# Mixture-of-experts tiles whose second matrix is read in place, by an address in a register

## The chip, the cores and the metric

The kernel runs on one core of a Trainium2 chip. A core has five engines with queues of their own: TensorE (PE: matmuls, with PEld for its weight loads), VectorE (DVE), ScalarE (ACT), GpSimd (POOL) and SyncE (SP, which only starts transfers). The metric is the device time of one execution in microseconds.

## The reference

The computation is a stack of six layers on `x`, four sequences of 512 tokens of width 128. Each layer is `x = x + c * f(layernorm(x))`. Attention layers have 16 heads of width 8, with or without a causal mask. Two of the feed-forward layers are a mixture of experts: each of the 2048 tokens picks one of eight experts and goes through that expert's two matrices.

```python
logits = hn2 @ gate_w + gate_b
idx = jnp.argmax(logits, axis=-1)
mid = jax.nn.relu(jnp.einsum('th,ehf->etf', hn2, w1) + b1[:, None, :])
y = jnp.einsum('etf,efh->eth', mid, w2) + b2[:, None, :]
moe = y[idx, jnp.arange(hn2.shape[0])]
return x + moe.reshape(b, s, h)
```

`w1` is 8 x 128 x 512 and `w2` is 8 x 512 x 128. The other two feed-forward layers are dense, with low-rank additions.

## The kernel before, in words

**Stages.** A "batch" in the code is one sequence in one layer: numbers 0 to 3 are the first attention layer (its feed-forward part is the first mixture), 4 to 7 the second (causal), 8 to 11 the third (the second mixture), 12 to 15 the fourth (causal). The mixture is done in four halves of two sequences, 1024 tokens each: halves 0 and 1 stand between batches 3 and 4, halves 2 and 3 between batches 11 and the dense layer before batch 12.

**One half.** `gate`, `pick`, `rank` and `place` find for each token its expert and its place in a list sorted by expert, with every expert's tokens rounded up to tiles of 128. Up to 15 tiles (`SLOTS`) result. `place` has three parts on VectorE: part 0 counts the tiles of each expert (four instructions from L1012), part 1 makes each token's position (`pos`, L1022 to L1030), part 2 writes `owner`, the expert number of each of the 15 tiles (L1033 to L1041). Eight indirect transfers on POOL (`scatter`, L1236) write the token rows, each with its token's number in a 129th column, into `sorted`. Two transfers on SP (`xload`, L1282 and L1283) bring the sorted rows back into `sorted_rows`.

**One tile** then goes through:

- `lay` (VectorE, L1049): copies the tile's expert, 1156 columns of `w1`, `w2`, `b1` and `b2` laid side by side, from the resident `experts` into one of `NWE` = 3 slots of `we`. The expert's number is in a register, which VectorE loads one tile ahead from `owner` (`expert_of`, L854: a load, a register instruction and an assertion that it is in bounds).
- `tt` (TensorE, L696) transposes the tile's rows; ScalarE applies the norm's scale and bias to `hTm` (L797).
- `up` (TensorE, L701): four matmul instructions with `w1` from `we`. The profile lists each fp32 instruction twice, so a group has 8. ScalarE applies relu with `b1` (L804).
- `dn` (TensorE, L707): four matmul instructions with `w2` from `we`. VectorE then waits for a free result slot out of `NY` = 8, copies the tile's token numbers into `numbers_y` (L1057) and adds `b2` into `ysb` (L1058).
- `ysend` (POOL, L1241) sends the result's rows to `y_rows` by an indirect transfer with `numbers_y` as index.

When all tiles of a half are sent, SP loads the rows back (`yload`, L1289) and VectorE adds them to `x` (`yadd`, L1063).

**Order.** `schedule` (L250) makes one list of events out of due times. Due times are in quads, where one quad is a quarter of a batch's attention; `TILES_AT`, `ROUTE_AT`, `Y_AT`, `NEXT`, `DENSE_AT` and others hold them. `segment` (L187) merges events by due time with the attention steps. Each engine's program (`pe_program` L587, `act_program`, `dve_program`, `pool_program`, `sync_program`) walks the same list and issues its own part of each event, so the list fixes the order within each queue, and semaphores do the rest. `need` issues a wait unless the engine has already waited for as much. `tile_before(n, at, k)` is the tile k places earlier, whose slot is used again.

In the list of before, half 1 has the parts of `place` in the order 1, 2, 0 by due time (part 0 is due at 19.259, part 1 at 18.75), all of half 1's lays stand behind half 0's last `dn`, and half 2's last `dn` stands behind the first `tt` of half 3. The events that begin batch 4 (`stats`, `rstd`, `norm`, then `hT`, L601, `q`, `k`, `v`) stand between the tiles of half 1, `hT` behind `dn` of tile 2.

Of the kernel before, what the change touches and what calls it, by code (L numbers as in the profile page):

```python
# [40 lines left out]
NWE = 3  # L41
NY = 8
FLIPS = TOPK
WE = 2 * F + FB + P
# [34 lines left out]
PREP = [('stats', 7.927), ('rstd', 7.55), ('norm', 7.1), ('hT', 6.9), ('q', 6.7), ('qrem', 6.65), ('k', 6.419),  # L79
        ('krem', 6.553), ('qmid', 6.3), ('kmid', 6.1), ('qlo', 6.05), ('klo', 5.851), ('v', 2.951), ('keep',  # L80
        -2.776)]
# [5 lines left out]
SECOND = [('hT', 1.871), ('q', 1.3), ('qrem', 1.25), ('k', 1.15), ('krem', 1.1), ('qmid', 1.0), ('kmid', 0.9),  # L87
        ('qlo', 0.94), ('klo', 0.8), ('v', -1.0), ('keep', -7.0)]
SECOND_STACK, SECOND_EVERY = 1.056, 0.182
# [3 lines left out]
        1.05), ('stats', 1, 1.2), ('rstd', 1, 1.2), ('norm', 1, 1.5), ('v', 0, 2.0)], 12: [('stats', 0, 0.207),  # L93
        ('rstd', 0, 0.0), ('norm', 0, 0.35), ('hT', 0, 0.5), ('q', 0, 0.65), ('qrem', 0, 0.7), ('k', 0, 0.8),
        ('krem', 0, 0.85), ('qmid', 0, 0.9), ('kmid', 0, 1.0), ('qlo', 0, 1.0), ('klo', 0, 1.05), ('stats', 1, 1.2),
        ('rstd', 1, 1.2), ('norm', 1, 1.5), ('v', 0, 3.334)]}
FLIP_AT = 15.132
# [4 lines left out]
STACK_FROM, STACK_EVERY = 6.412, 0.253  # L102
# [3 lines left out]
LOADS_FROM, LOADS_EVERY = 2.931, 0.418  # L106
# [6 lines left out]
        13.45, 'xfold': 13.65, 'lnorm': 13.9, 'lT': 14.4, 'gate': 14.8}, 3: {'lstats': 17.25, 'lrstd': 17.25,  # L113
# [7 lines left out]
        'lnorm': 6.3, 'lT': 6.8}, 13: {'lstats': 9.85, 'lrstd': 9.85, 'lnorm': 10.3, 'lT': 10.8}, 14: {'lstats':  # L121
        15.25, 'lrstd': 15.25, 'lnorm': 15.7, 'lT': 16.2}, 15: {'lstats': 17.65, 'lrstd': 17.48, 'lnorm': 17.88,
        'lT': 18.13}}
ROUTE_AT = {0: {'pick': 11.1, 'rank': 11.6, 'place0': 11.8, 'place1': 12.0, 'place2': 12.2, 'scatter': 12.209,
        'every': 0.15, 'xload': 15.2}, 1: {'pick': 18.304, 'rank': 18.5, 'place0': 19.259, 'place1': 18.75,
        'place2': 18.95, 'scatter': 18.8, 'every': 0.005, 'xload': 20.0}, 2: {'pick': 27.1, 'rank': 27.6, 'place0':
        27.8, 'place1': 28.189, 'place2': 28.389, 'scatter': 28.3, 'every': 0.15, 'xload': 31.2}, 3: {'pick': 34.2,
        'rank': 34.5, 'place0': 34.55, 'place1': 34.598, 'place2': 34.9, 'scatter': 34.362, 'every': 0.005, 'xload':
        36.0}}
# [5 lines left out]
Y_AT = {0: {'yload': 20.072, 'yadd0': 20.582, 'yadd1': 20.682}, 1: {'yload': 23.882, 'yadd0': -0.468, 'yadd1':  # L135
        -0.221}, 2: {'yload': 36.197, 'yadd0': 36.597, 'yadd1': 36.697}, 3: {'yload': 39.75, 'yadd0': 40.093,
        'yadd1': 40.123}}
DENSE_AT = {8: {'at': 39.75, 'unit': 0.26, 'fdn': 1.05}, 9: {'at': 40.764, 'unit': 0.273, 'fdn': 1.063}, 10: {'at':
        41.843, 'unit': 0.273, 'fdn': 1.011}, 11: {'at': 44.011, 'unit': 0.221, 'fdn': 1.05}, 12: {'at': 14.2,
        'unit': 0.121, 'fdn': 1.05, 'send': 1.3}, 13: {'at': 15.391, 'unit': 0.26, 'fdn': 1.05, 'send': 1.3}, 14:  # L140
        {'at': 16.9, 'unit': 0.26, 'fdn': 1.05, 'send': 1.3}, 15: {'at': 18.4, 'unit': 0.26, 'fdn': 1.05, 'send':
        1.3}}
NEXT_AT = {4: {'at': 20.651, 'stack': 0.801, 'every': 0.152}, 12: {'at': 41.47, 'stack': 0.801, 'every': 0.136}}


def tiles_of(hm):

    T, jobs = TILES_AT[hm], []
    for t in range(SLOTS):
        up = T["start"] + T["every"] * t  # L150
        jobs += [(up - (T["lay0"] if t < 2 else T["lay"]), "lay", hm, t), (up + T["tt"], "tt", hm, t),
                 (up, "up", hm, t), (up + T["dn"], "dn", hm, t), (up + T["ysend"], "ysend", hm, t)]
    return jobs
# [13 lines left out]
def sums(hm):  # L167
    return [(Y_AT[hm][f"yadd{b}"], "yadd", 2 * hm + b, None) for b in range(2)]

# [79 lines left out]

def schedule(causal_of):  # L250
# [22 lines left out]
    return plan + segment([12, 13, 14, 15], causal_of, jobs)  # L273


def program(nc, d):
    with ExitStack() as ctx:
# [63 lines left out]
        experts = sb("experts", [P, E, WE])  # L341
# [23 lines left out]
        numbers_y = sb("numbers_y", [P, NY], U32)  # L365
# [187 lines left out]
        def number_of(hm, t):  # L553
            return hm * SLOTS + t
# [31 lines left out]

        def pe_program(pe):  # L587
            for ev in plan:
# [108 lines left out]
                elif name == "up":  # L697
                    need(pe, b_free, at_b[("tt", n, at)] + 1)
# [30 lines left out]
        def act_program(a):  # L729
            for ev in plan:  # L730
# [68 lines left out]
                elif name == "up":  # L799
                    if tile_before(n, at, 2):  # L800
                        need(a, a_full, at_a[("dn", *tile_before(n, at, 2))] + 1)
                    for fb in range(FB):
                        at_ = number_of(n, at) % NWE
                        ins = a.activation(mid_e[:, number_of(n, at) % 2, fb, :], b_tiles(o)[:, fb, :], ACT.Relu,  # L804
                                           bias=we[:, at_, 2 * F + fb:2 * F + fb + 1])
# [33 lines left out]
        def dve_program(v):  # L839
# [11 lines left out]
            def expert_of(eng, hm, t):  # L851

                k_ = SLOTS * (hm % 2) + t
                return eng.value_load(owner[0:1, k_:k_ + 1], min_val=0, max_val=E - 1)  # L854

            next_expert = {}
            for ev in plan:
# [173 lines left out]
                elif name == "place":  # L1031
# [11 lines left out]
                    next_expert[n] = expert_of(v, n, 0)  # L1043
                elif name == "lay":
# [4 lines left out]
                    v.tensor_copy(we[:, number_of(n, at) % NWE, :], experts[:, bass.ds(next_expert[n], 1), :]  # L1049
                                  .rearrange("p o c -> p (o c)")).then_inc(laid, 1)  # L1050
                    if at + 1 < SLOTS:
                        next_expert[n] = expert_of(v, n, at + 1)
                elif name == "dn":
                    r = number_of(n, at) % NY
                    if tile_before(n, at, NY):
                        need(v, y_sent[r], 16 * (number_of(n, at) // NY))
                    v.tensor_copy(numbers_y[:, r:r + 1], sorted_rows[n % 2][:, at, P:ROW].bitcast(U32))  # L1057
                    v.tensor_tensor(ysb[:, r, :], pair_of(ka)[:, 0, 0:P],  # L1058
                                    we[:, number_of(n, at) % NWE, 2 * F + FB:WE], ALU.add).then_inc(a_free, 1)
# [94 lines left out]
        def pool_program(g_):  # L1154
            for ev in plan:
# [274 lines left out]
```

## Time and profile before

| | us |
|---|---|
| median of 3 runs | 1014.93 |
| lowest and highest | 1014.77, 1016.52 |
| the profiled execution | 1020.19 |
| its span (first to last instruction) | 1018.4 |
| TensorE busy in the span | 897.5 |
| VectorE busy in the span | 779.7 |
| ScalarE busy in the span | 674.8 |

The profile is of one execution, 5.26 us above the median; its granted TensorE clock averages 0.966 of full speed. Times of rows are counted from the start of the span. In a row of an engine's list, the bracket behind it gives the idle time of that engine before it and what ended the idle time; an arrow points from what is written to what is read. "issue" means that the profile shows nothing that the engine waited for, and "remote" or "another core or an unknown queue" that the event which released it has no visible source.

### The profile page before, as it was taken

The numbers are of one execution on the slowest core, as the hardware profiler recorded it, in microseconds if no ns is written. First come the engines' busy times: TensorE is split into PE (matmuls) and PEld (weight loads), VectorE is DVE, ScalarE is ACT, GpSimd is POOL, SyncE is SP. The second block draws the span as 40 slices with busy tenths as digits, with TensorE's granted clock in tenths as the row PEclk, the third lists the DMA queues.
The fourth block names the chain that finished last, engine by engine and source line by source line (L and its number), as shares of the span: only waits on it lengthen the run. The fifth ranks groups of instructions, "written<-read, shape, count | busy, mean of one in ns | idle before, by whom it ended". The sixth has DMA issues, their size and how long they took to land.

```text
span 1018.4 us, 25342 instructions
## 1 busy us (share of the span) xinstructions
PE 897.5 (88%) x10020; PEld 477.1 (47%) x10020; DVE 779.7 (77%) x1412; ACT 674.8 (66%) x1470; POOL 342.2 (34%) x603
## 2 busy tenths in 40 slices
PE   2699999898778799999899999889698989999998
PEld 1123333236767455554323333249685645555465
DVE  5889899855447887888989999817368788888646
ACT  2288887786555577777798878786362358767631
POOL 4444312242646323233232312516571133311100
PEclk8599999999989899999999999999799989999999
DMA  5117740001133221121010200010310222110000
GB/s 146 46 44 178 191 107 2 16 10 47 43 94 85 78 66 35 35 66 43 23 46 22 55 11 2 23 41 30 97 33 24 62 64 65 33 38 4 3 22 21
DMA packets 60520, 52.29 MB, mean 51 GB/s; under 512 B 9106, under 2 KB 57362, under 8 KB 60402
## 3 DMA queue, kind: packets, MB, share of 16 engines
q1 hardware_dynamic: 48980, 40.00, 14.6%
q10 hardware_dynamic: 8478, 4.62, 2.2%
q0 software_dynamic: 2944, 6.05, 1.8%
q8 instruction: 79, 1.29, 0.6%
q14 instruction: 39, 0.32, 0.1%
HBM read 13.64 MB, written 11.06 MB: 24 GB/s over the span
## 4 chain that ended last, share of the span: by engine, by line
PE 53%; DVE 21%; issue 10%; ACT 10%; another core or an unknown queue 2%; DMA 2%; POOL 1%; DVEq 1%; ACTq 0%; SPq 0%; POOLq 0%
PE ps L576 14%; PE ps L652 13%; DVE negm L937 10%; ACT pt L770 7%; PE ps L715 4%; PE ps L607 3%; PE ps L707 3%; PE ps L701 3%; PE ps L582 3%; DVE blockm L928 2%; PE ps L721 2%; PE ps L660 2%; PE ps L612 1%; PE ps L670 1%
## 5 line engine op out<-in xcount | busy, mean ns | idle before, releaser
L770 ACT ACTIVATE pt<-ps 128x512 f32<-128x512 f32 (+1 forms) x896 | 458.3, 567 | 156.1 <-PE ps L576 107.2
L937 DVE TENSOR_REDUCE negm<-ps 128x2 f32<-128x1024 f32 x256 | 300.9, 1219 | 31.0 <-PE ps L576 28.4
L652 PE MATMUL ps<-pt,va 128*32 128x256 f32 (+1 forms) x4352 | 274.3, 341 | 12.1 <-ACT ot L776 5.5
L928 DVE TENSOR_REDUCE blockm<-ps 128x8 f32<-128x1024 f32 (+1 forms) x192 | 195.2, 1042 | 34.2 <-PE ps L576 21.8
L576 PE MATMUL ps<-ks,qs 61*128 61x128 bf16 (+2 forms) x1536 | 174.0, 293 | 35.7 <-DVE negm L937 16.0
L576 PE MATMUL ps<-qs,ks 64*128 64x128 bf16 (+3 forms) x1408 | 168.1, 296 | 7.8 <-ACT pt L770 2.3
L652 PEld LDWEIGHTS ps<-pt,va 128*32 128x32 f32 x4352 | 91.9, 108 | 124.5 <-issue 83.0
L576 PEld LDWEIGHTS ps<-ks,qs 61*128 61x128 bf16 x1536 | 54.8, 95 | 189.8 <-issue 86.6
L1206 POOL CAST mpart<-negm 128x16 bf16<-128x16 f32 x64 | 13.2, 207 | 300.2 <-DVE negm L937 153.8
L804 ACT ACTIVATE stage<-ps,pt 128x128 f32<-128x128 f32 x240 | 68.6, 373 | 41.6 <-PE ps L701 29.8
L1241 POOL DMA_INDIRECT y_rows<-pt,numbers_y x60 | 70.7, 1179 | 63.4 <-DVE pt L1058 55.0
L576 PEld LDWEIGHTS ps<-qs,ks 64*128 64x128 bf16 x1408 | 57.9, 94 | 63.7 <-ACT pt L770 47.0
L701 PE MATMUL ps<-hTm,pt 128*128 128x128 f32 x480 | 68.0, 287 | 15.0 <-DVE pt L1049 12.9
L707 PE MATMUL ps<-pt,stage 128*128 128x128 f32 x480 | 66.5, 283 | 4.5 <-ACT stage L804 3.4
L701 PEld LDWEIGHTS ps<-hTm,pt 128*128 128x128 f32 x480 | 61.4, 200 | 19.0 <-ACT hTm L797 12.0
L1146 POOL TENSOR_TENSOR q<-q,parts 128x512 f32<-128x512 f32 x29 | 33.5, 1156 | 95.0 <-ACT parts L752 94.9
L1049 DVE COPY pt<-experts 128x1156 f32 x60 | 46.7, 785 | 24.0 <-PE ps L652 17.6
L707 PEld LDWEIGHTS ps<-pt,stage 128*128 128x128 f32 x480 | 61.0, 199 | 6.1 <-issue 4.5
L715 PE MATMUL ps<-hTa,wk 128*128 128x512 f32 x128 | 58.6, 599 | 2.3 <-DVE stage L1070 1.6
L810 ACT ACTIVATE stage<-ps 128x512 f32<-128x512 f32 x32 | 19.1, 597 | 37.2 <-PE ps L715 32.4
L797 ACT ACTIVATE hTm<-ps,wpk 128x128 f32<-128x128 f32 x60 | 28.2, 472 | 21.2 <-remote 12.3
L607 PE MATMUL ps<-hT,wpk 128*128 128x512 f32 x64 | 39.0, 699 | 1.7 <-ACT hT L743 0.9
(151 smaller groups left out, 1017.9 us busy)
## 6 DMA issues: line engine op xcount, KB each, us to landing
qs<-parts SPq DMA_DIRECT2D x80, 128.0 KB
ks<-parts SPq DMA_DIRECT2D x77, 128.0 KB
experts<-in_experts SPq DMA_DIRECT2D x8, 578.0 KB, 6.3
sorted<-stage ACTq DMA_DIRECT2D x4, 967.5 KB, 8.3
qs<-mrow SPq DMA_DIRECT2D x128, 6.0 KB
pt<-y_rows SPq DMA_DIRECT2D x8, 256.0 KB, 2.9
qs<-parts SPq DMA_DIRECT2D x32, 56.0 KB
ks<-parts SPq DMA_DIRECT2D x30, 56.0 KB
```

The source lines that it names most:

```text
L576: ends[s] = pe.matmul(banks[s][:, col:col + c1 - c0], stationary[s][:, i * P:(i + 1) * P], moving[s][:, c0:c1], start=(m_ == 0), stop=(not ...
L607: pe.matmul(b_bank(o), w["w" + name], hT[:, :], start=True, stop=True).then_inc(b_full, 1)
L652: ins = pe.matmul(pv_bank[32 * j:32 * j + 32, q0:q1], va[n % 2][:, kb, value_at(g, j):value_at(g, j) + 32], pt[:, k_, from_:from_ + q1 - q ...
L701: ins = pe.matmul(b_tiles(o)[:, a, :], we[:, number_of(n, at) % NWE, a * P:(a + 1) * P], hTm[:, number_of(n, at) % 2, :], start=True, stop ...
L707: ins = pe.matmul(pair_of(ka)[:, 0, 0:P], mid_e[:, number_of(n, at) % 2, a, :], we[:, number_of(n, at) % NWE, F + a * P:F + (a + 1) * P], ...
L715: pe.matmul(pair_of(ka)[:, 0, :] if kx else b_bank(o), wk[:, kx, at * P:(at + 1) * P], hTa[:, n % 2, :], start=True, stop=True).then_inc(a ...
L770: a.activation(pt[:, k_ % NPT, S * s:S * s + width], b_bank(o + s)[:, 0:width], ACT.Exp).then_inc(b_free, 1)
L804: ins = a.activation(mid_e[:, number_of(n, at) % 2, fb, :], b_tiles(o)[:, fb, :], ACT.Relu, bias=we[:, at_, 2 * F + fb:2 * F + fb + 1])
L928: v.tensor_reduce(blockm[:, g % 2, :, t, PLACES[c_]], pair_of(ka)[:, :, 0:width].rearrange("p s (b c) -> p s b c", c=P), AX, ALU.max, nega ...
L937: v.tensor_reduce(negm[:, g % 2, :, t, c_], pair_of(ka), AX, ALU.max, negate=True).then_inc(a_free, 1)
L1049: v.tensor_copy(we[:, number_of(n, at) % NWE, :], experts[:, bass.ds(next_expert[n], 1), :] .rearrange("p o c -> p (o c)")).then_inc(laid, 1)
L1241: g_.indirect_dma_start(d["y_rows"][n], bass.IndirectOffsetOnAxis(numbers_y[:, r:r + 1], 0), ysb[:, r, :], None).then_inc(y_sent[r], 16)
```

## The change

The second matrix is no longer copied by `lay`. It stays in `experts`, and each `dn` matmul reads it there at an address that is worked out from a register. For that, TensorE loads all 15 expert numbers of a half in one go, ahead of the half's first `up`; VectorE does the same at the end of `place` part 2, in place of one number per tile. `lay` copies 644 columns into one of 5 slots. Results have 15 slots, one for each tile of a half, and `numbers_y` goes: `ysend` reads the index straight from the 129th column of `sorted_rows`. The load of half 2's sorted rows therefore waits until half 0's results have been sent. The weights are packed in another order on the host, with the same bytes. A check at build time (`in_order`) fixes the order of the routing steps and of the counted events, and the due times are set anew.

```diff
-NWE = 3
-NY = 8
+NWE = 5
+NY = SLOTS
-WE = 2 * F + FB + P
+WE = F + FB + P
+W2_AT = WE
...
-        experts = sb("experts", [P, E, WE])
+        experts = sb("experts", [P, E, WE + F])
...
+        def experts_of(engine, hm):
+
+            k_ = SLOTS * (hm % 2)
+            return nc.values_load_multi_w_load_instructions(owner[0:1, k_:k_ + SLOTS], engines=[engine], min_val=0,
+                                                            max_val=E - 1)[1]
...
                 elif name == "up":
+                    if at == 0:
+                        need(pe, owner_step, 3 * n + 3)
+                        expert[n] = experts_of(mybir.EngineType.PE, n)
...
                     for a in range(FB):
+                        w2 = experts[:, bass.ds(expert[n][at], 1), W2_AT + a * P:W2_AT + (a + 1) * P]
                         ins = pe.matmul(pair_of(ka)[:, 0, 0:P], mid_e[:, number_of(n, at) % 2, a, :],
-                                        we[:, number_of(n, at) % NWE, F + a * P:F + (a + 1) * P], start=(a == 0),
-                                        stop=(a == FB - 1))
+                                        w2.rearrange("p o c -> p (o c)"), start=(a == 0), stop=(a == FB - 1))
...
                     v.wait_ge(owner_step, 3 * n + 3)
-                    next_expert[n] = expert_of(v, n, 0)
+                    expert[n] = experts_of(mybir.EngineType.DVE, n)
...
-                    v.tensor_copy(we[:, number_of(n, at) % NWE, :], experts[:, bass.ds(next_expert[n], 1), :]
+                    v.tensor_copy(we[:, number_of(n, at) % NWE, :], experts[:, bass.ds(expert[n][at], 1), 0:WE]
                                   .rearrange("p o c -> p (o c)")).then_inc(laid, 1)
-                    if at + 1 < SLOTS:
-                        next_expert[n] = expert_of(v, n, at + 1)
...
-                    v.tensor_copy(numbers_y[:, r:r + 1], sorted_rows[n % 2][:, at, P:ROW].bitcast(U32))
...
-                    g_.indirect_dma_start(d["y_rows"][n], bass.IndirectOffsetOnAxis(numbers_y[:, r:r + 1], 0),
+                    g_.indirect_dma_start(d["y_rows"][n], bass.IndirectOffsetOnAxis(sorted_rows[n % 2][:, at, P:ROW]
+                                                                                      .bitcast(U32), 0),
...
                     elif n == 2:
-                        need(sp, a_free, at_a[("dn", 0, SLOTS - 1)] + 1)
+                        for r in range(NY):
+                            need(sp, y_sent[r], 16 * len(range(r, SLOTS, NY)))
```

What the due times move, in the order of the list: half 0's lays run two tiles earlier; half 1's `place` goes in the order 0, 1, 2; its first lays stand ahead of half 0's last `dn`; batch 4's `hT` stands behind `dn` of tile 4, `k` behind tile 5, `v` behind tile 12; half 2's last `dn` stands ahead of half 3's first `tt`. The rest, shown in part, moves by a tile or a step of attention at most:

```diff
-        1.05), ('stats', 1, 1.2), ('rstd', 1, 1.2), ('norm', 1, 1.5), ('v', 0, 2.0)], 12: [('stats', 0, 0.207),
+        1.05), ('stats', 1, 1.2), ('rstd', 1, 1.2), ('norm', 1, 1.5), ('v', 0, 2.267)], 12: [('stats', 0, 0.207),
-LOADS_FROM, LOADS_EVERY = 2.931, 0.418
+LOADS_FROM, LOADS_EVERY = 2.751, 0.418
-        'rank': 34.5, 'place0': 34.55, 'place1': 34.598, 'place2': 34.9, 'scatter': 34.362, 'every': 0.005, 'xload':
+        'rank': 34.5, 'place0': 34.55, 'place1': 34.58, 'place2': 34.9, 'scatter': 34.362, 'every': 0.005, 'xload':
-TILES_AT = {0: {'start': 16.75, 'every': 0.207, 'lay0': 0.35, 'lay': 0.384, 'tt': -0.257, 'dn': 0.22699999999999998,
-        'ysend': 0.277}, 1: {'start': 20.401, 'every': 0.207, 'lay0': 0.35, 'lay': 0.384, 'tt': -0.213, 'dn':
-        0.22699999999999998, 'ysend': 0.216}, 2: {'start': 32.681, 'every': 0.207, 'lay0': 0.35, 'lay': 0.214, 'tt':
+TILES_AT = {0: {'start': 16.75, 'every': 0.207, 'lay0': 0.35, 'lay': 0.719, 'tt': -0.257, 'dn': 0.22699999999999998,
+        'ysend': 0.277}, 1: {'start': 20.088, 'every': 0.207, 'lay0': 0.358, 'lay': 0.392, 'tt': -0.213, 'dn':
+        0.22699999999999998, 'ysend': 0.216}, 2: {'start': 32.628, 'every': 0.207, 'lay0': 0.35, 'lay': 0.304, 'tt':
-        'lay': 0.363, 'tt': -0.257, 'dn': 0.22699999999999998, 'ysend': 0.277}}
+        'lay': 0.268, 'tt': -0.257, 'dn': 0.22699999999999998, 'ysend': 0.548}}
```

## Rows read from the trace of the kernel before

**Rows 1.** The profile page: the engines' busy time, the chain by engine.
```profile
PE 897.5 (88%) x10020; PEld 477.1 (47%) x10020; DVE 779.7 (77%) x1412; ACT 674.8 (66%) x1470; POOL 342.2 (34%) x603
...
PE 53%; DVE 21%; issue 10%; ACT 10%; another core or an unknown queue 2%; DMA 2%; POOL 1%; DVEq 1%; ACTq 0%; SPq 0%; POOLq 0%
```

**Rows 2.** Table of windows: busy us of each engine, clock, DMA share, GB/s.
```profile
270.00:290.00 20.00, 10.74 (x61) 9.62 (x62) 5.76 (x17) 5.46 (x19) 11.47 (x12) 0.74 0.31 93
290.00:326.00 36.00, 31.08 (x258) 28.63 (x258) 22.34 (x73) 23.94 (x75) 23.82 (x20) 1.00 0.29 82
...
712.00:732.00 20.00, 11.13 (x67) 10.25 (x66) 4.45 (x12) 6.19 (x21) 12.01 (x12) 0.78 0.32 94
```

**Rows 3.** Table of waits: engine, line, releaser; us in total, times, longest.
```profile
DVE numbers_y L1057 <- remote: 16.2, 5, 6.1
...
PE ps L701 <- DVE pt L1049: 12.9, 9, 4.2
```

**Rows 4.** Engine lists, half 0 into 1: start, us, work, [idle before <- releaser].
```profile
259.79 1.46 POOL L1241 DMA_INDIRECT y_rows<-pt,numbers_y  x1 [1.33 <-DVE pt L1058]
...
270.87 1.13 PE L701 MATMUL ps<-hTm,pt 128*128 128x128 f32 x8 [1.01 <-DVE pt L1049]
...
273.79 0.68 PE L701 MATMUL ps<-hTm,pt 128*128 128x128 f32 x4 [0.90 <-DVE pt L1049]
...
279.27 2.04 PE L707 MATMUL ps<-pt,stage 128*128 128x128 f32 x8 [3.20 <-ACT stage L804]
...
285.10 0.15 DVE L1057 COPY numbers_y<-stage 128x1 uint32<-128x1 uint32 x1 [2.52 <-remote]
...
286.27 2.04 PE L701 MATMUL ps<-hTm,pt 128*128 128x128 f32 x8 [4.22 <-DVE pt L1049]
```

**Rows 5.** Instructions of L1049, then of L1057: ns least/median/most.
```profile
L1049 DVEq FUSED_REGOPS  x60: 57/57/65, 238.8 to 756.8; - x60
L1049 DVE COPY pt<-experts x60: 730/763/1552, 238.9 to 756.9; 128x1156 f32 x60
...
L1057 DVE COPY numbers_y<-stage x30: 145/154/155, 244.4 to 727.9; 128x1 uint32<-128x1 uint32 x30
```

**Rows 6.** VectorE's list at place0; POOL's behind half 1's last scatter.
```profile
271.75 0.21 DVE L1012 SCALAR_TENSOR_TENSOR more<-ranks,count 128x64 f32<-128x64 f32 x1
...
277.30 0.96 POOL L1241 DMA_INDIRECT y_rows<-pt,numbers_y  x1 [0.30 <-issue]
...
285.73 1.22 POOL L1241 DMA_INDIRECT y_rows<-pt,numbers_y  x1 [1.92 <-DVE pt L1058]
```

**Rows 7.** TensorE's list: batch 4's first transposes, between tiles of half 1.
```profile
297.78 0.66 PE L601 MATMUL ps<-identf,lnx 128*128 128x128 f32 x4 [2.38 <-DVE lnx L897]
```

**Rows 8.** TensorE's list, half 2 into half 3.
```profile
721.71 0.47 PE L696 MATMUL ps<-identf,pt 128*128 128x128 f32 x1 [5.67 <-DMA pt<-sorted]
...
721.98 1.92 PE L707 MATMUL ps<-pt,stage 128*128 128x128 f32 x8
...
729.08 1.34 PE L701 MATMUL ps<-hTm,pt 128*128 128x128 f32 x8 [3.04 <-DVE pt L1049]
```

**Rows 9.** The chain of waits behind half 2's place part 2: start, us, what.
```profile
641.42 0.31 DVEq L854
...
641.77 0.19 DVEq L854
...
642.00 0.02 DVEq L854
...
642.06 0.36 DVE rc L945
```

**Rows 10.** Engine lists: behind half 0's place part 2, and its first up.
```profile
195.41 2.36 DVE L937 TENSOR_REDUCE negm<-ps 128x2 f32<-128x1024 f32 x2 [0.95 <-DVE owner L1041]
...
240.03 1.06 PE L701 MATMUL ps<-hTm,pt 128*128 128x128 f32 x8
```

**Rows 11.** The chain of waits, half 2 into half 3.
```profile
715.45 6.05 another core or an unknown queue
```

More of the change, by code:

```diff
@@ L77 @@
 LEAD = 2.0
[L79 to L81 removed]
+PREP = [('stats', 7.927), ('rstd', 7.55), ('norm', 7.1), ('hT', 6.967), ('q', 6.767), ('qrem', 6.717), ('k', 6.486),
+        ('krem', 6.62), ('qmid', 6.3), ('kmid', 6.1), ('qlo', 6.05), ('klo', 5.851), ('v', 2.951), ('keep', -2.776)]
 HEAD = [("stats", 0), ("rstd", 0), ("norm", 0), ("stats", 1), ("rstd", 1), ("clear", 0), ("hT", 0), ("q", 0), ("qrem", 0),
@@ L124 @@
+        'lnorm': 17.88, 'lT': 18.13}}
 ROUTE_AT = {0: {'pick': 11.1, 'rank': 11.6, 'place0': 11.8, 'place1': 12.0, 'place2': 12.2, 'scatter': 12.209,
-        'every': 0.15, 'xload': 15.2}, 1: {'pick': 18.304, 'rank': 18.5, 'place0': 19.259, 'place1': 18.75,
-        'place2': 18.95, 'scatter': 18.8, 'every': 0.005, 'xload': 20.0}, 2: {'pick': 27.1, 'rank': 27.6, 'place0':
-        27.8, 'place1': 28.189, 'place2': 28.389, 'scatter': 28.3, 'every': 0.15, 'xload': 31.2}, 3: {'pick': 34.2,
-        'rank': 34.5, 'place0': 34.55, 'place1': 34.598, 'place2': 34.9, 'scatter': 34.362, 'every': 0.005, 'xload':
+        'every': 0.15, 'xload': 15.2}, 1: {'pick': 18.304, 'rank': 18.5, 'place0': 18.7, 'place1': 18.75, 'place2':
@@ L129 @@
+        18.95, 'scatter': 18.8, 'every': 0.005, 'xload': 20.0}, 2: {'pick': 27.1, 'rank': 27.6, 'place0': 27.8,
+        'place1': 28.189, 'place2': 28.389, 'scatter': 28.3, 'every': 0.15, 'xload': 31.2}, 3: {'pick': 34.2,
+        'rank': 34.5, 'place0': 34.55, 'place1': 34.58, 'place2': 34.9, 'scatter': 34.362, 'every': 0.005, 'xload':
         36.0}}
-TILES_AT = {0: {'start': 16.75, 'every': 0.207, 'lay0': 0.35, 'lay': 0.384, 'tt': -0.257, 'dn': 0.22699999999999998,
-        'ysend': 0.277}, 1: {'start': 20.401, 'every': 0.207, 'lay0': 0.35, 'lay': 0.384, 'tt': -0.213, 'dn':
-        0.22699999999999998, 'ysend': 0.216}, 2: {'start': 32.681, 'every': 0.207, 'lay0': 0.35, 'lay': 0.214, 'tt':
+TILES_AT = {0: {'start': 16.75, 'every': 0.207, 'lay0': 0.35, 'lay': 0.719, 'tt': -0.257, 'dn': 0.22699999999999998,
+        'ysend': 0.277}, 1: {'start': 20.088, 'every': 0.207, 'lay0': 0.358, 'lay': 0.392, 'tt': -0.213, 'dn':
+        0.22699999999999998, 'ysend': 0.216}, 2: {'start': 32.628, 'every': 0.207, 'lay0': 0.35, 'lay': 0.304, 'tt':
@@ L143 @@
-NEXT_AT = {4: {'at': 20.651, 'stack': 0.801, 'every': 0.152}, 12: {'at': 41.47, 'stack': 0.801, 'every': 0.136}}
+        'lay': 0.268, 'tt': -0.257, 'dn': 0.22699999999999998, 'ysend': 0.548}}
+Y_AT = {0: {'yload': 20.072, 'yadd0': 20.275, 'yadd1': 20.682}, 1: {'yload': 23.882, 'yadd0': -0.225, 'yadd1':
+        -0.221}, 2: {'yload': 36.143, 'yadd0': 36.543, 'yadd1': 36.776}, 3: {'yload': 39.79, 'yadd0': 40.05,
+        'yadd1': 40.069}}
+DENSE_AT = {8: {'at': 39.531, 'unit': 0.004, 'fdn': 0.794}, 9: {'at': 40.764, 'unit': 0.273, 'fdn': 1.063}, 10:
+        {'at': 41.843, 'unit': 0.273, 'fdn': 1.011}, 11: {'at': 44.011, 'unit': 0.221, 'fdn': 1.05}, 12: {'at':
+        14.096, 'unit': 0.121, 'fdn': 1.05, 'send': 1.3}, 13: {'at': 15.645, 'unit': 0.26, 'fdn': 1.05, 'send':
+        1.3}, 14: {'at': 16.9, 'unit': 0.26, 'fdn': 1.05, 'send': 1.3}, 15: {'at': 18.141, 'unit': 0.26, 'fdn':
+        1.05, 'send': 1.3}}
@@ L146, in tiles_of @@
+NEXT_AT = {4: {'at': 20.651, 'stack': 0.803, 'every': 0.152}, 12: {'at': 41.47, 'stack': 0.801, 'every': 0.136}}
 def tiles_of(hm):
-    T, jobs = TILES_AT[hm], []
+    T, jobs, lay = TILES_AT[hm], [], -NEVER
     for t in range(SLOTS):
         up = T["start"] + T["every"] * t
-        jobs += [(up - (T["lay0"] if t < 2 else T["lay"]), "lay", hm, t), (up + T["tt"], "tt", hm, t),
+        lay = max(lay, up - (T["lay0"] if t < 2 else T["lay"]))
+        jobs += [(lay, "lay", hm, t), (up + T["tt"], "tt", hm, t),
@@ L167, in sums @@
 def sums(hm):
-    return [(Y_AT[hm][f"yadd{b}"], "yadd", 2 * hm + b, None) for b in range(2)]
+    Y = Y_AT[hm]
+    return [(max(Y["yadd0"], Y[f"yadd{b}"]), "yadd", 2 * hm + b, None) for b in range(2)]
 def norms(l):
@@ L247, in segment, with in_order @@
     return out
+ROUTING = [("gate", 0), ("gate", 1), ("pick", None), ("rank", None), ("place", 0), ("place", 1), ("place", 2)]
+COUNTED = ("lay", "tt", "up", "dn", "xfold", "yadd", "lstats", "lrstd", "lnorm", "stats", "rstd", "norm", "keep", "out")
+def in_order(plan):
+    at = {ev: i for i, ev in enumerate(plan) if ev[0] in ("gate", "pick", "rank", "place")}
+    steps = [("gate", 2 * hm + k, None) if name == "gate" else (name, hm, k) for hm in range(4) for name, k in ROUTING]
+    assert all(at[a] < at[b] for a, b in zip(steps, steps[1:]))
+    for name in COUNTED:
+        counted = [ev[1:] for ev in plan if ev[0] == name]
+        assert counted == sorted(counted, key=lambda ev: (ev[0], ev[1] or 0)), (name, counted)
+    return plan
 def schedule(causal_of):
@@ L585, in score_pieces @@
             return ends
+        def experts_of(engine, hm):
+            k_ = SLOTS * (hm % 2)
+            return nc.values_load_multi_w_load_instructions(owner[0:1, k_:k_ + SLOTS], engines=[engine], min_val=0,
+                                                            max_val=E - 1)[1]
         def pe_program(pe):
+            expert = {}
             for ev in plan:
@@ L849, in over_e @@
                 return t[:, :].rearrange("p (i o) -> p i o", o=1).broadcast_to([P, TILES, E])
[L851 to L856, printed above, removed]
+            expert = {}
             for ev in plan:
```

38 lines of the change are left out of this document (14 added, 24 removed).

## The prediction

> **What bounds the kernel now.** I read the page first: TensorE is busy for 88% of the span, and over half of the chain of waits that ended last is its own work [rows 1]. The attention segments make up most of that, and the change leaves them nearly alone. So I went to the four expert stages by a table of windows. Inside a stage TensorE is almost solid and runs at the full clock; the time is lost where one half gives way to the next, 270 to 290 us and 712 to 732 us, where TensorE works for about 11 of 20 us and the granted clock averages 0.74 and 0.78 [rows 2]. The table of waits then names the causes: TensorE waited 12.9 us for the lay copies, nine times, and VectorE 16.2 us for something the profile calls remote [rows 3]. The engines' lists show whether the nine are steady or singular: 1.01, 0.90, 4.22 and 3.04 us of them stand at the two boundaries [rows 4, 8]; the other five share the remaining 3.7.
>
> The "remote" waits need care. They stand before the numbers_y copy, the first instruction after a wait for a free result slot, which suggests that eight slots are too few. But the copy at 285.10 is tile 14's, its slot was tile 6's, and POOL sent that at 259.79; TensorE began tile 14's group at 279.27 and ended it at 281.31 [rows 4]. What came late was the word from TensorE's matmuls. Fifteen slots in place of eight are therefore worth **nothing** by themselves here.
>
> **The change part by part.**
>
> *Lay copy.* A 1156-column copy takes 0.763 us and a one-column copy 0.154 [rows 5]. On the line between them 644 columns take 0.154 + 0.557 x 0.609 = 0.49 us, 0.27 less: 16 us of VectorE's time over 60 tiles. Each tile also loses its numbers_y copy (0.15 us) and a register load with its check, 0.31 + 0.19 + 0.02 us and gaps, 0.64 us as the chain has it [rows 9], most of that behind the running copy. Of this only what TensorE waits for counts. With five slots and earlier due times the lays stand two tiles ahead in half 0, and the 3.7 us of scattered waits should go: **-3.7**, bounds 0 and -12.9 (all nine).
>
> *First boundary.* Half 1's place0 (four VectorE steps, about 1.0 us from 271.75) now stands ahead of place1, so the scatters start some 0.7 us later. Against that, POOL's tail can close up: behind the last scatter ysends run 1.26 us apart (0.96 and an idle 0.30) from 277.30, so six of them would start their last at 277.30 + 5 x 1.26 = 283.6, where it started at 285.73 because VectorE's add was late [rows 6]. The lays of half 1 no longer stand behind that add in VectorE's queue. The rows go back 2.1 - 0.7 = 1.4 us earlier, and what waits for them is the sum, then batch 4's statistics, norm and hT [rows 7]: **-1.4**, bounds 0 and -4.2 (TensorE's whole lay wait at 286.27 [rows 4]).
>
> *hT of batch 4.* TensorE waits 2.38 us for lnx with the remaining tiles queued behind hT's four transposes [rows 7]. hT now follows dn(1,4) in place of dn(1,2), k and v later still; their matmuls, evacuations and stack DMAs go along. Two tiles (an up and a dn group of about 1.06 us each [rows 10]) are longer than the wait: **-2.4**, bounds 0 and -2.4.
>
> *Second boundary.* dn(2,14) stood behind tt(3,0), which waits 5.67 us for the sorted rows; dn, its add and its ysend now go ahead. VectorE's queue held lays behind that add: up(3,1) waited 3.04 us for them [rows 8]: **-3.0**, bounds 0 and -5.7 (all of the wait for the sorted rows).
>
> *The load of fifteen numbers, on VectorE in place2.* No row shows one. A single number takes 0.64 us from load to next instruction: 0.31 the load, 0.33 the check with its gaps [rows 9]. Ends: 0.64 (the check is paid once) and 15 x 0.64 = 9.6 us. I take one full set and 14 short ones of 0.057 + 0.02, from the lay's own register instruction [rows 5] and the assertion [rows 9], which together is 0.64 + 14 x 0.08 = 1.8, or 1.1 more than now. It is exposed twice (halves 0 and 2, on the chain with negm or the reciprocals right behind [rows 9, 10]): **+2.2**. In halves 1 and 3 it falls into the boundary.
>
> *The same load on TensorE.* It stands ahead of up(n,0). In halves 0 and 2 TensorE runs there without a gap ([rows 10], 240.03), so 1.8 us counts, twice: **+3.6**, bounds 2 x 0.64 and 2 x 9.6. In half 1 it lies under the wait that ends at 286.27 [rows 4]; in half 3 between 0 and 1.8, taken as nothing because hTm of tile 0 is on its way meanwhile.
>
> *Register addresses of dn.* 240 matmul instructions, each with a register instruction of 0.057 [rows 5] on TensorE's queue: 13.7 us if exposed. Each covers 0.265 us of array work, so the queue can run ahead: 0, bounds 0 and +13.7.
>
> *The rest.* xload of half 2 waits for fifteen semaphores in place of one, at a time when they have long been counted; yload for fifteen in place of eight, the last now being the last sent. Expert loads move 0.18 quad earlier, and no row shows anyone waiting for them. Preparations, norms, yadds and dense units move by a tile at most, with stack DMAs on SP's queue moving with them. Together 0, bounds -4 and +4, the size of one of the larger waits above.
>
> **Sum**: -3.7 - 1.4 - 2.4 - 3.0 + 2.2 + 3.6 = -4.7 us. The profiled execution took 1020.19 us, 1.79 of it outside its span, and lies 5.26 above the median 1014.93. 1020.19 - 4.7 = 1015.5 there, or **1010.2** as a median.
>
> **Rivals.**
>
> *Every number pays a full check (slower).* Place: the two loads. Then one takes 0.31 + 15 x 0.33 = 5.3 us; VectorE pays 2 x 4.6 and TensorE 2 x 5.3, 19.8 in all against 10.5 of gains: +9.3, **1024**. It decides from a load of L = 2.95 us on (2 x L + 2 x (L - 0.64) = 10.5). For it: a check of 0.19 us is more than three of the lay's register instructions of 0.057 [rows 5, 9], so it looks like work and not like waiting. Against: the fifteen share one load, and checks may be folded together. In this rival TensorE would also cool: after the waits of 4.22 and 5.67 us the matmul groups took 2.04 and 1.92 us, at half the clock [rows 4, 8]. The Trainium skill ("TensorE: Matmul & The Clock Gate", section "Why this matters for your kernels") advises against idle gaps between bursts for this reason; the trace agrees in both boundaries. By that rule two more such stretches, each with four groups some 0.98 us longer than the 1.06 of [rows 10], would add 7.8 and make it 1032.
>
> *The register addresses break TensorE's stream.* 13.7 us on top of the forecast: **1024**. Against it: the weight loads and matmuls leave the queue as much time as the array.
>
> *The late words vanish.* The chain puts 2%, some 20 us, down to an unknown queue [rows 1]; the longest piece of it, 6.05 us, is at the second boundary [rows 11]. If the new order of POOL's work halves the 20: 1010.2 - 10 = **1000**.
>
> *No change.* POOL's indirect DMAs set both boundaries, 1.26 us apart whatever the other engines do; then only 3.7 + 2.4 of the gains remain, 6.1 against 5.8: **1014.6**.
>
> **How the numbers follow.** About 0.2% (2 us) is what a measurement of this kernel can tell from no change. Forecast 0.43, late words vanish 0.16: faster 0.59. No change 0.12. Full checks 0.22 (0.06 of it with the clock fallen as well), register addresses 0.07: slower 0.29. I predict 1010.2; the range 998 to 1025 reaches to the rivals at 1000 and 1024 and leaves out the fallen clock and two of the far bounds. The likeliest case alone spans 1004 to 1013.
>
> **What would show it.** Right: lay copies near 0.49 us and gone from TensorE's waits but for the boundaries; one register load per half on each of the two engines lasting under 2.5 us; dn groups still 1.06 us; no 2.38 wait ahead of hT; POOL's ysends 1.26 apart up to the last of half 0. Wrong: fifteen checks of 0.19 in a row ahead of up(0,0) and after place2, with TensorE idle and the clock lower behind them; dn groups above 1.06; or remote waits of VectorE and ScalarE at the boundaries that grow or shrink by several us.

## The result, and the profile after

The changed kernel takes 1045.24 us (median of 4 runs, 1044.53 to 1045.86) against 1015.72 for the kernel before: a ratio of 1.029, 95% interval 1.0273 to 1.0308. That is 29.5 us slower, where 4.7 us faster was forecast, and outside the range of 998 to 1025. Of all executions behind the numbers from here on one, of the kernel with 13 result slots, took 1202.62 us at a granted clock of 0.65, and its time is left out.

The page of the changed kernel shows no engine with much more work. TensorE is busy for 5 us longer than in [rows 1], VectorE for 22 us less, and the lay copy takes 0.50 us in place of 0.76:

```profile
PE 902.5 (87%) x10020; PEld 484.6 (46%) x10020; DVE 757.2 (73%) x1352; ACT 673.8 (65%) x1470; POOL 329.5 (32%) x603
...
PE 56%; DVE 20%; ACT 9%; issue 9%; DVEq 2%; POOL 2%; DMA 1%; ACTq 0%; POOLq 0%
...
L1072 DVE COPY pt<-experts 128x644 f32 x60 | 29.5, 500 | 24.3 <-PE ps L677 23.5
```

So the span of 1043.0 us holds more waiting. The table of waits says where. In [rows 3] TensorE's largest wait inside a tile was for the lay copies. Now it is one for nothing that the profile knows ("issue"), four times and up to 7.4 us long, and VectorE's add has two such waits:

```profile
PE ps L729 <- issue: 25.5, 4, 7.4
...
DVE pt L1078 <- issue: 16.0, 2, 8.2
```

What the two queues did in that time is in the instructions of the line that loads the expert numbers, L608 (ns: least, median, most; then the first and last start):

```profile
L608 DVEq FUSED_REGOPS  x60: 183/183/206, 194.0 to 738.0; - x60
L608 DVEq SEQ_ASSERT  x60: 23/23/41, 194.3 to 738.2; - x60
L608 PEldq FUSED_REGOPS  x60: 146/146/165, 244.5 to 754.2; - x60
L608 PEldq SEQ_ASSERT  x60: 18/18/28, 244.7 to 754.4; - x60
L608 DVEq TENSOR_LOAD <-owner x4: 1666/2720/3582, 192.1 to 730.6; - x4
L608 PEldq TENSOR_LOAD <-owner x4: 1582/2696/3852, 242.7 to 746.5; - x4
```

The change does load once per half: four loads on each engine. But such a load takes 1.6 to 3.9 us where the load of one number took 0.31 [rows 9], and the checks were not folded together: VectorE still has 60 and TensorE has 60 more, now in rows of fifteen. The chain of waits behind half 0's place part 2 shows the row of them begin; [rows 9] has the same place of half 2 in the kernel before:

```profile
191.86 0.17 DVE owner L1064
192.06 1.92 DVEq L608
193.98 0.04 issue
194.02 0.21 DVEq L608
...
194.26 0.04 DVEq L608
...
194.33 0.19 DVEq L608
...
197.91 0.18 DVEq L608
...
198.20 1.24 DVE negm L960
```

From 192.06 to 198.16 VectorE's queue does nothing else: 6.1 us, with 0.275 us from one check to the next. TensorE waits for the negm behind it. From first load to last assertion the eight loads take 6.1, 8.1, 6.2 and 7.7 us on VectorE and 6.2, 8.1, 5.9 and 7.9 on TensorE (halves 0 to 3): 56 us. The engines' lists show what stood behind them, in order of time:

```profile
199.48 1.11 PE L685 MATMUL ps<-identf,ot 128*128 128x128 f32 x4 [7.20 <-DVE negm L960]
...
249.06 2.05 PE L729 MATMUL ps<-hTm,pt 128*128 128x128 f32 x8 [5.68 <-issue]
...
285.65 0.49 DVE L1078 TENSOR_TENSOR pt<-ps,pt 128x128 f32<-128x128 f32 x2 [8.18 <-issue]
286.10 2.07 PE L736 MATMUL ps<-experts,stage 128*128 x8 [6.40 <-DVE pt L1078]
...
300.04 2.05 PE L729 MATMUL ps<-hTm,pt 128*128 128x128 f32 x8 [7.36 <-issue]
...
739.18 2.05 PE L729 MATMUL ps<-hTm,pt 128*128 128x128 f32 x8 [5.94 <-DVE pt L1072]
...
754.58 2.05 PE L729 MATMUL ps<-hTm,pt 128*128 128x128 f32 x8 [7.14 <-issue]
```

At 249.06 stands the first up of half 0, which came without a gap in [rows 10]. At 285.65 VectorE returns to half 0's adds after its load for half 1, and TensorE's dn had waited 6.40 us for a free accumulator; the up at 739.18 waited in the same way behind VectorE's load for half 3. What these two waits cost on balance, the section on both edits shows. Each up or dn group that follows such a wait takes 2.05 to 2.07 us in place of 1.06: the clock had fallen. The table of windows has it near the level of 1.2 GHz (0.5; full speed, 1.0, is 2.4 GHz) right behind two of the loads:

```profile
199.00:206.00 7.00, 6.52 (x40) 2.26 (x40) 4.86 (x7) 2.50 (x5) 0.00 (x0) 0.54 0.00 1
...
249.00:254.00 5.00, 4.78 (x24) 4.41 (x25) 0.00 (x0) 2.04 (x7) 0.00 (x0) 0.58 0.00 0
```

### The profile page after: what moved, and what is told of

It reads as the page before. It is cut to its first block, busy times and chain, and to the rows that moved or that the text cites. A ratio compares the mean times of both kernels' runs of the same rounds, so it can differ in the third digit from the quotient of the medians.

```text
span 1043.0 us, 25597 instructions
## 1 busy us (share of the span) xinstructions
PE 902.5 (87%) x10020; PEld 484.6 (46%) x10020; DVE 757.2 (73%) x1352; ACT 673.8 (65%) x1470; POOL 329.5 (32%) x603
## 3 DMA queue, kind: packets, MB, share of 16 engines
q1 hardware_dynamic: 48980, 40.00, 14.3%
## 4 chain that ended last, share of the span: by engine, by line
PE 56%; DVE 20%; ACT 9%; issue 9%; DVEq 2%; POOL 2%; DMA 1%; ACTq 0%; POOLq 0%
PE ps L594 14%; PE ps L677 13%; DVE negm L960 9%; ACT pt L798 7%; PE ps L729 5%; PE ps L743 4%; PE ps L736 4%; DVE blockm L951 3%; PE ps L600 3%; PE ps L632 2%; DVEq L608 2%; PE ps L749 2%; PE ps L685 2%; PE ps L695 1%; PE ps L637 1%
## 5 line engine op out<-in xcount | busy, mean ns | idle before, releaser
L594 PE MATMUL ps<-ks,qs 61*128 61x128 bf16 (+2 forms) x1536 | 174.3, 293 | 36.6 <-DVE negm L960 17.2
L729 PE MATMUL ps<-hTm,pt 128*128 128x128 f32 x480 | 73.5, 303 | 33.3 <-issue 25.5
L1078 DVE TENSOR_TENSOR pt<-ps,pt 128x128 f32<-128x128 f32 x60 | 17.2, 289 | 98.3 <-PE ps L736 82.0
L729 PEld LDWEIGHTS ps<-hTm,pt 128*128 128x128 f32 x480 | 66.7, 215 | 36.6 <-issue 32.9
L736 PE MATMUL ps<-experts,stage 128*128 x480 | 66.9, 285 | 8.1 <-DVE pt L1078 7.9
L736 PEld LDWEIGHTS ps<-experts,stage 128*128 128x128 f32 x480 | 61.4, 200 | 9.3 <-issue 9.2
L1072 DVE COPY pt<-experts 128x644 f32 x60 | 29.5, 500 | 24.3 <-PE ps L677 23.5
L838 ACT ACTIVATE stage<-ps 128x512 f32<-128x512 f32 x32 | 19.1, 598 | 38.9 <-PE ps L743 37.5
L1261 POOL DMA_INDIRECT y_rows<-pt,stage x30 | 29.9, 997 | 45.0 <-DVE pt L1078 40.0
L1261 POOL DMA_INDIRECT y_rows<-pt x30 | 29.8, 992 | 40.8 <-DVE pt L1078 37.1
```

Of the source, the lines that this page charges most:

```text
L594: ends[s] = pe.matmul(banks[s][:, col:col + c1 - c0], stationary[s][:, i * P:(i + 1) * P], moving[s][:, c0:c1], start=(m_ == 0), stop=(not ...
L729: ins = pe.matmul(b_tiles(o)[:, a, :], we[:, number_of(n, at) % NWE, a * P:(a + 1) * P], hTm[:, number_of(n, at) % 2, :], start=True, stop ...
```

## The experiments

All are timed against the kernel before on the same chip, whose median lay between 1015.5 and 1016.3 us in them.

**Loads without checks.** Only the bounds checks are left out.

```diff
-            return nc.values_load_multi_w_load_instructions(owner[0:1, k_:k_ + SLOTS], engines=[engine], min_val=0,
-                                                            max_val=E - 1)[1]
+            return nc.values_load_multi_w_load_instructions(owner[0:1, k_:k_ + SLOTS], engines=[engine], min_val=0,
+                                                            max_val=E - 1, skip_runtime_bounds_check_because=
+                                                            "owner counts the experts that end before a tile")[1]
```

> The changed kernel, but the fifteen numbers are loaded without the bounds check of each. Theory 1 (the loads of fifteen numbers cost the time): a load's 15 checks take 15 x 0.275 = 4.1 us on VectorE and about the same on TensorE, 8 loads; the 4 in halves 0 and 2 are exposed in full (-16.6) and those at the two boundaries in part (-8 to -12), so 1017 to 1021. What is left of a load is 1.7 to 3.6 us. Theory 2 (register addresses of dn and the new order cost the time, the loads fall into waits that were there anyway): not below 1033. Theory 3 (the clock that falls behind each load is the larger part of the loss): a load of 2 us no longer lets the clock fall, so more than 8 x 4.1 = 33 us come back, below 1012.

Measured: 1012.09 us, ratio 0.9962 (0.9948 to 0.9976), 33.2 us less than the changed kernel. That is 5 us below Theory 1's range and just short of Theory 3's bound. The checks of the eight loads last 34.6 us together, so by its size alone the number does not tell whether all eight stood in the way. The traces do, by where the time came back. From the end of place part 2 to the first up of halves 0 and 2, where four of the loads lie, 18.2 us came back for 17.4 us of checks; from there to the last dn of halves 1 and 3, where the other four lie, 13.1 for 17.2. So the checks cost their length in the first place and three quarters of it at the boundaries. Theory 3's premise does not hold: behind the load of 1.9 us that is left in half 0 the granted clock is still 0.66 in 195 to 199 us. What remains of the loads is one instruction each:

```profile
L608 DVEq TENSOR_LOAD <-owner x4: 1679/2740/3608, 192.7 to 705.1; - x4
L608 PEldq TENSOR_LOAD <-owner x4: 1587/2804/3898, 238.0 to 718.6; - x4
```

**One number per tile, on TensorE.** The load for a tile's dn stands behind that tile's up.

```diff
                 elif name == "up":
                     if at == 0:
                         need(pe, owner_step, 3 * n + 3)
-                        expert[n] = experts_of(mybir.EngineType.PE, n)
...
                     ins.then_inc(b_full, 1)
+                    expert[n, at] = expert_of(pe, n, at)
```

> The changed kernel, but TensorE loads one number per tile, right behind that tile's up matmuls, in place of fifteen ahead of a half's first up. Theory 1: the waits of 5.7, 7.4, about 7 and 7.1 us ahead of the first up of each half go, less what other work at the boundaries then ends last: -18 to -25, so 1020 to 1027; the single loads (about 0.6 us) run under the 1.06 us of up. Theory 2: nothing is won, since 60 single loads of 0.6 us (36 us) now stand in TensorE's queue: 1040 or more.

Measured: 1016.25 us, ratio 1.0004 (0.9992 to 1.0016), 29.0 us less than the changed kernel. That is 4 us more than Theory 1 had at most, and as much as TensorE's four loads last (28.2 us): all four stood in the way in full.

**One number ahead per tile, on VectorE,** as the kernel before does.

```diff
-                    expert[n] = experts_of(mybir.EngineType.DVE, n)
+                    expert[n, 0] = expert_of(v, n, 0)
...
                                   .rearrange("p o c -> p (o c)")).then_inc(laid, 1)
+                    if at + 1 < SLOTS:
+                        expert[n, at + 1] = expert_of(v, n, at + 1)
```

> The changed kernel, but VectorE loads one number ahead per tile, as the kernel before does, in place of fifteen in place part 2. Theory 1: 5.4 and 5.5 us go in halves 0 and 2, and at the boundaries the waits of TensorE for VectorE's late add (6.4 and 5.9 us): -17 to -23, so 1022 to 1028. Theory 2: at most the 11 us of halves 0 and 2, 1034 or more, because the boundaries wait for POOL's transfers anyway.

Measured: 1027.96 us, ratio 1.0116 (1.0095 to 1.0137), 17.3 us less: Theory 1, at the lower end of its gain. VectorE's four loads last 28.0 us, so some of that had been hidden.

**Both edits together.**

> The changed kernel with one number per tile on both engines. Theory 1: the gains of the two single edits add up, less some 5 us at the boundaries where the two loads stand behind each other: 1000 to 1008, below the kernel before (1015.7), which would be what the rest of the change is worth. Theory 2: the rest of the change costs time by itself: 1016 or more.

Measured: 999.83 us, ratio 0.984 (0.9821 to 0.9859). The gains add up almost fully (29.0 + 17.3 = 46.3; 45.4 measured). The rest of the change is worth 16 us, and Theory 2 has fallen. Where the gains lie, the four profiled executions show against that of the changed kernel (us). The first stretch runs from the end of place part 2 to the first up, in halves 0 and 2; the second from there to the last dn of halves 1 and 3, with the boundaries in it:

| | first stretch: the loads there | came back | second stretch: the loads there | came back |
|---|---|---|---|---|
| without checks (of the loads, the checks) | 17.4 | 18.2 | 17.2 | 13.1 |
| one number per tile on TensorE | 12.1 | 11.1 | 16.0 | 17.1 |
| one number per tile on VectorE | 12.3 | 14.3 | 15.8 | **2.4** |
| both | 24.4 | 25.6 | 31.8 | 19.1 |

The rest of the span differs by some 0.6 us at most. So TensorE's loads cost about their length in both stretches, VectorE's a little more than theirs in halves 0 and 2, and at the boundaries next to nothing. When they go from there, another wait takes their place, the one for half 1's and half 3's sorted rows. The table of waits has it with VectorE's single numbers and with both edits (in this order), and does not have it in the changed kernel, where the rows had come by the time VectorE let TensorE go on:

```profile
PE ps L726 <- DMA pt<-sorted: 11.7, 2, 6.8
```

```profile
PE ps L726 <- DMA pt<-sorted: 12.1, 2, 7.5
```

TensorE's own load is not covered by that wait, because it is in the queue behind the transposes that wait for the rows. With VectorE's single numbers the rows come at 284.07, and half 1's first up, behind TensorE's load, starts 8.2 us later:

```profile
284.07 0.69 PE L726 MATMUL ps<-identf,pt 128*128 128x128 f32 x2 [6.85 <-DMA pt<-sorted]
292.31 2.05 PE L734 MATMUL ps<-hTm,pt 128*128 128x128 f32 x8 [7.55 <-issue]
```

With both edits the same 120 numbers are loaded and checked as in the changed kernel, one at a time, and TensorE's matmuls show no wait for theirs. The instructions of that load's line and of dn's, and TensorE's list in half 0:

```profile
L614 PEldq TENSOR_LOAD <-owner x60: 296/301/572, 236.7 to 738.0; - x60
L614 PEldq FUSED_REGOPS  x60: 151/151/165, 237.2 to 738.4; - x60
...
L741 PEldq FUSED_REGOPS  x240: 46/46/65, 239.9 to 741.5; - x120
```

```profile
236.91 1.06 PE L733 MATMUL ps<-hTm,pt 128*128 128x128 f32 x8
...
242.98 1.06 PE L741 MATMUL ps<-experts,stage 128*128 x8
243.87 0.27 PE L726 MATMUL ps<-identf,stage 128*128 128x128 f32 x1
243.98 1.06 PE L733 MATMUL ps<-hTm,pt 128*128 128x128 f32 x8
244.88 1.06 PE L741 MATMUL ps<-experts,stage 128*128 x8
```

TensorE's queue does 0.3 + 0.15 + 0.02 us for the number and 4 x 0.046 for the addresses in each tile, and the array shows no gap: from one dn to the next it is 1.90 us. The groups take 1.06 as in [rows 10].

**The same, unchecked.** 

> One number per tile on both engines, and none of them checked against its bounds. If single loads run under other work (Theory 1), only the two in place part 2 that stand on the chain become shorter: 998 to 1000, against 999.8 with the checks. If they are exposed on TensorE's queue tile by tile, 60 checks of about 0.2 us go: 985 to 990.

Measured: 998.36 us, ratio 0.9825 (0.9794 to 0.9855), 1.5 less than with checks, a step that the intervals do not separate. The checks of single numbers are hidden, but for those of the first number of a half in place part 2: in half 0 TensorE's wait behind it falls from 1.98 to 1.67 us.

**VectorE's load of fifteen moved to the first lay.** Nothing is taken out.

```diff
-                    v.wait_ge(owner_step, 3 * n + 3)
-                    expert[n] = experts_of(mybir.EngineType.DVE, n)
                 elif name == "lay":
                     need(v, experts_loaded, 16 * E)
+                    if at == 0:
+                        v.wait_ge(owner_step, 3 * n + 3)
+                        expert[n] = experts_of(mybir.EngineType.DVE, n)
```

> The changed kernel, fifteen numbers at once on both engines and all checked, but VectorE's load stands ahead of a half's first lay and no longer at the end of place part 2. Nothing is removed, one thing is moved: in halves 0 and 2 VectorE waits 11.8 us for TensorE's last attention matmuls ahead of the first lay, so a load of 6.1 us that started a little earlier would be covered, though the wait itself stands behind the load. Theory 1 (a load costs what it covers or does not cover): the 5.4 and 5.5 us of halves 0 and 2 go, and the boundaries gain 0 to 6, since fewer adds of half 0 and 2 stand behind the load: 1028 to 1034. If the loss hung on the load's length alone, wherever it stands: 1045.

Measured: 1022.12 us, ratio 1.0063 (1.0042 to 1.0084), 23.1 less than the changed kernel and more than I expected. The load of half 0 now runs from 221.19 to 227.17, while VectorE has nothing to do, and its first lay still waits for TensorE's matmuls only. VectorE's list there, TensorE's where it had waited 7.20 us, and the window where the changed kernel had the low clock:

```profile
233.00 0.50 DVE L1073 COPY pt<-experts 128x644 f32 x1 [11.70 <-PE ps L677]
```

```profile
192.96 0.66 PE L685 MATMUL ps<-identf,ot 128*128 128x128 f32 x4 [0.93 <-DVE negm L960]
```

```profile
199.00:206.00 7.00, 6.87 (x71) 2.51 (x70) 6.54 (x8) 5.42 (x12) 4.96 (x8) 1.00 0.07 22
```

From the end of place part 2 to the first up it now takes 48.3 us (half 0) and 44.1 (half 2), where it took 57.0 and 52.9. That is 8.8 and 8.7 us, though the load that left this place took 6.1 and 6.2. In half 0 TensorE's wait is 6.3 us shorter (0.93 for 7.20); the other 2.5 us had gone at half the clock behind the stall: from that matmul to the first one of L695 it is 5.8 us here and was 8.3.

**Slots, structure and timetable.** Four more kernels split the 16 us. First, the kernel before with 13 result slots (`NY = 13`) and nothing else:

> The kernel before with 13 result slots in place of 8 (15 do not fit beside its wide lay slots), nothing else. Theory A (the prediction's: the waits at the boundaries that the profile calls remote are not waits for a slot): 1016 within 2 us, and the remote waits of VectorE and ScalarE are there again, 20 us or more. Theory B (they come from the slots): they go, and the time falls to 1006 to 1012.

Measured: 1016.75 us, ratio 1.002 (0.9998 to 1.0042). More slots are worth nothing, as Theory A has it. Yet the remote waits were gone, which Theory A did not have, and without the gain that Theory B had for it. So the kernel before was profiled again:

> The kernel before, unchanged, profiled once more. If the remote waits of VectorE and ScalarE at the boundaries (39 us in the table of waits of the first profile) belong to the kernel, they are there again and the span is about 1018; if they belonged to that one execution, they are gone and the span is 1013 to 1015.

Measured: 1015.49 us, span 1013.7. There is no remote wait in the table, and the lay waits are 7.6 us where [rows 3] had 12.9:

```profile
DVE numbers_y L1057 <- PE ps L707: 46.9, 34, 7.5
...
PE ps L701 <- DVE pt L1049: 7.6, 7, 2.3
```

The remote waits belonged to the one execution that the prediction was read from, which was 5.26 us over the median. What delayed it isn't known. Of its two long lay waits at the boundaries, 4.22 and 3.04 us [rows 4, 8], the second profile has neither.

Then the changed kernel with single numbers but the old due times (apart from half 1's place part 0), and the old kernel with the new due times (half 0's lay lead at its old 0.384):

> The changed kernel with one number per tile on both engines, and with the due times of the kernel before, but for half 1's place part 0, which stays ahead of part 1. It has the new structure (second matrix read in place, 5 and 15 slots, no numbers_y) without the new timetable. Theory C (the structure brings most of the 16 us that this version gains over the kernel before): 1000 to 1006. Theory D (the timetable does): 1010 to 1016.

> The kernel before with the due times of the changed one, but half 0's lays not two tiles earlier, since three slots do not allow that. Theory C: 1010 to 1016, the timetable alone brings little. Theory D: 1000 to 1006. The terms of the prediction that belong to the timetable (hT 2.4, the second boundary 3.0, the first boundary in part) would give 1009 to 1011.

| | old due times | new due times |
|---|---|---|
| old structure | 1015.5 | 1006.81 (0.991, 0.9879 to 0.994) |
| new structure, single numbers | 1010.0 (0.9943, 0.9924 to 0.9963) | 999.83 (0.984, 0.9821 to 0.9859) |

1010.0 lies at the edge of Theory D's range and 1006.81 between the two: the timetable brings more than half, 8.7 us alone or 10.2 on top of the structure, the structure 5.5 alone or 7.0, and together 16. Most of the timetable's gain lies in attention, where I had priced it at nothing. From half 1's last dn to the end of half 2's place part 2 it is 315.5 us in the kernel before (316.8 in its second profile) and 312.5 with the new due times; from the start to half 0's, 194.5 (193.7) and 192.6; from half 3's last dn to the end, 256.4 (256.7) and 255.0. Against the second profile that is 7.1 us; the expert stages in between gained 1.7 and 0.4.

Last, the old kernel with the new due times, 13 slots and no numbers_y copy:

```diff
-                    v.tensor_copy(numbers_y[:, r:r + 1], sorted_rows[n % 2][:, at, P:ROW].bitcast(U32))
...
-                    g_.indirect_dma_start(d["y_rows"][n], bass.IndirectOffsetOnAxis(numbers_y[:, r:r + 1], 0),
+                    g_.indirect_dma_start(d["y_rows"][n], bass.IndirectOffsetOnAxis(sorted_rows[n % 2][:, at, P:ROW]
+                                                                                      .bitcast(U32), 0),
```

> The kernel before with the new due times, with 13 result slots and without the numbers_y copy (the index is read from the sorted rows), but lay still copies both matrices into three slots and dn reads the copy. Against 1006.8 with the due times alone this prices slots and numbers_y, and what is then left to 999.8 is worth of the short lay, five slots and the second matrix read in place. The prediction's terms (slots nothing, numbers_y hidden but for a part, lay waits 3.7): 1005 to 1007. If the copy stood on the path of each tile: 60 x 0.15 = 9 us, 998.

Measured: 1006.53 us, ratio 0.9912 (0.9884 to 0.994), against 1006.81: slots and numbers_y are worth nothing here either. The 6.7 us from there to 999.83 belong to the short lay, five slots and the second matrix read in place, together. TensorE's wait for lays, first with the old structure and the new due times, then with both new:

```profile
PE ps L700 <- DVE pt L1048: 5.9, 7, 1.6
```

```profile
PE ps L733 <- DVE pt L1077: 0.8, 1, 0.8
```

**The best version.** Single numbers without checks, and VectorE's first one of a half ahead of the first lay:

> One number per tile on both engines without checks, and VectorE's first number of a half loaded ahead of the first lay in place of place part 2. The 0.3 to 0.5 us of that load leave the chain in halves 0 and 2: 997 to 998.4, against 998.4 with the load in place part 2.

Measured: 995.63 us, ratio 0.9801 (0.9775 to 0.9827). It beats both kernels, by 2% and 4.7%. The step from 998.36 is 2.7 us, more than the two short loads last. 2.1 of them lie between half 0's place part 2 and its first up. TensorE's wait behind place part 2 is 0.93 us there in place of 1.67, and the clock no longer falls behind it. The windows, first with the load in place part 2, then without it:

```profile
192.00:199.00 7.00, 5.22 (x36) 1.83 (x34) 5.71 (x9) 3.32 (x8) 3.51 (x4) 0.77 0.13 41
```

```profile
192.00:199.00 7.00, 5.89 (x58) 2.11 (x58) 6.53 (x10) 4.78 (x11) 3.63 (x4) 1.00 0.15 48
```

So a single number there had cost clock as well, in the kernel before too: its second profile has a wait of 1.99 us in this place and a granted clock of 0.81 in the same window.

## Why the prediction was wrong

**The step that failed** is the price of the load: "I take one full set and 14 short ones of 0.057 + 0.02 ... which together is 0.64 + 14 x 0.08 = 1.8". It measured 5.9 to 8.1. A check is work of 0.15 to 0.18 us for every number, and the load ahead of the checks grows as well, from 0.31 to between 1.6 and 3.9 us. The two ends of the bound were 0.64 and 9.6, and I took a value near the lower one on the strength of a register instruction of another kind. The row that was nearest in kind was the check itself, 0.19 us [rows 9], as I wrote under the first rival.

**Half of the second step** failed too, the overlap at the boundaries. It failed for TensorE: "it lies under the wait that ends at 286.27" and "taken as nothing". TensorE's load is in its queue behind the transposes that wait for the sorted rows, so it begins when the old wait is over, and its 16.0 us at the two boundaries came back in full (17.1). It held for VectorE: "In halves 1 and 3 it falls into the boundary". The waits behind VectorE's load (6.40 us at 286.10) look expensive in the trace, but they took the place of the wait for the sorted rows, and 2.4 us came back for 15.8. So six loads of eight counted, where the prediction had four.

**The first rival** had the mechanism and the sign, with both errors in its price: 5.3 us and four loads gave 1024. The eight loads last 56 us as measured, and 45.4 came back: nearly all but VectorE's at the boundaries. The sentence on the clock held: groups of twice their length stand behind the stalls in the list above. Where it could be separated, it cost 2.5 us beside a wait that was 6.3 us longer.

**What held.** The lay copy: 0.49 us forecast, 0.488 measured. Register addresses of dn: hidden, 0.046 us each. Slots: nothing. numbers_y: nothing. hT's wait of 2.38 us went with the new order, but left one of 0.9 for ScalarE's hT behind it.

**What was too small.** The rest of the change is worth 16 us, not 10.5. The structure's lay term of 3.7 measured 5.5 (old due times) or 6.7 to 7.0 (new ones). The timetable's terms, 1.4 + 2.4 + 3.0 = 6.8, measured 8.7, but not where I had put them: "The rest ... Together 0" gave 3 to 4 us in one attention segment and 1 to 2 in each of two others, and the expert stages, for which the three terms were worked out, gained some 2 us. That the sum of the terms comes near the measured gain is luck.

**A reading that didn't hold.** The rival "the late words vanish" rested on the remote waits of one execution; they weren't a property of the kernel. That the slots don't explain them was right. The terms of the two boundaries were read from the same execution, with lay waits of 4.22 and 3.04 us that the second profile does not have.

## What to carry to other kernels

Count what a batched load issues per element, not per call: loading fifteen checked numbers at once was fifteen checks in a row, and everything behind them in that queue stood for 5.9 to 8.1 us. TensorE's 60 loads were free one per tile, in the shadow of a 1 us matmul group, and VectorE's four were free as a batch where the engine was waiting anyway. A long wait behind such a load is not yet its price: take the load away and see which other wait appears in its place. Before pricing a wait from one profile, see whether that execution's own time lies near the median.

## What the runs showed that I had not expected

- A load of fifteen numbers took 1.5 to 1.9 us in halves 0 and 2 and 3.5 to 3.9 at the boundaries, on both engines, in the changed kernel and in the two experiments that kept both loads. POOL's indirect transfers run at the boundaries, but they also run during VectorE's short loads at 192 and 650 us, and single loads at the boundaries still took mostly 0.30. The loads of halves 1 and 3 differ also in what they read, the numbers 15 to 29 of `owner` and not the first fifteen. No run separates the two, and the cause stays open.
- A stall of VectorE in the middle of attention cost 8.8 us where the load itself took 6.1: the stretch behind it ran at half the clock (granted 0.54 in 199 to 206 us, 1.00 without the stall). Behind a wait of 1.67 us in the same place the clock fell as well (0.77 in 192 to 199 us), behind one of 0.93 it did not (1.00).
- The queue of TensorE can take a register load, its check and four address computations per tile of 1.9 us, some 0.65 us in all, without a gap in the array.
